# The rows of x of two attentions, transposed by TensorE or by DMA

## The reference

```
x = layernorm(x + causal_attention(x))          # weights with low-rank additions, output projection
h = ln1(x + self_attention(x));                  # "self": queries, keys, values all from x
h = ln2(h + cross_attention(h, context))
h = ln3(h + relu(h @ fc1 + b1) @ fc2 + b2)
x = layernorm(x + h)
x = layernorm(x + bit_ffn(x))                    # quantized activations and weights, gelu
```

## Time and profile before

| | us |
|---|---|
| median of 3 runs | 3415.64 (3407.46 to 3430.44) |
| profiled execution, its own time | 3414.83 |
| its span, first to last instruction | 3413.0 |
| mean granted TensorE clock | 0.974 of full speed |

### The profile page before, as it was taken

The page is one execution under the profiler, slowest core; times in us unless marked ns, Lnnn a source line. Parts: engine busy times, 40 slices in busy tenths (PEclk is TensorE's granted clock), DMA queues, the critical chain, the costliest instruction groups (busy, mean ns, idle before and its releaser), DMA issues.

```text
span 3413.0 us, 88599 instructions
## 1 busy us (share of the span) xinstructions
PE 3142.6 (92%) x35500; PEld 2438.5 (71%) x35500; DVE 2618.3 (77%) x4755; ACT 1999.8 (59%) x4522; POOL 1227.4 (36%) x1128
## 2 busy tenths in 40 slices
PE   7999999998999869999999999999989999999996
PEld 4888888877889747777777777777765656556562
DVE  5777788888889758888888888888875666666666
ACT  2665566666667626667677666667773444435442
POOL 0444421136665652443344333334212222222122
PEclk9999999999999889999999999999999999999998
DMA  3566655436554544555445545554343112221212
GB/s 99 171 185 217 184 156 161 135 116 196 160 164 136 161 118 119 125 130 127 119 123 133 129 121 126 129 124 107 84 153 105 48 49 53 50 53 44 54 38 52
DMA packets 445189, 405.71 MB, mean 119 GB/s; under 512 B 270471, under 2 KB 352523, under 8 KB 443630
## 3 DMA queue, kind: packets, MB, share of 16 engines
q1 hardware_dynamic: 444526, 399.78, 43.3%
q10 hardware_dynamic: 256, 0.26, 0.0%
HBM read 239.72 MB, written 109.52 MB: 102 GB/s over the span
## 4 chain that ended last, share of the span: by engine, by line
PE 55%; DMA 13%; DVE 13%; SPq 8%; ACT 5%; issue 4%; POOL 1%; ACTq 0%; POOLq 0%; DVEq 0%
PE at_ps L746 23%; PE at_ps L890 5%; PE at_ps L870 4%; PE at_ps L833 4%; PE at_ps L1393 4%; PE at_ps L1407 3%; DMA causal_spill<-at_proj 3%; PE at_ps L1418 3%; DMA self_spill<-at_proj 3%; PE at_ps L1372 2%; DVE at_mx_cross L953 2%; SPq L702 2%; DMA at_w_first<-cross_spill 2%; DMA at_o_raw<-at_values 2%; PE at_ps L775 2%
## 5 line engine op out<-in xcount | busy, mean ns | idle before, releaser
L960 DVE TENSOR_TENSOR at_p<-at_ps,at_p 125x448 f16<-125x448 f32 (+1 forms) x1280 | 781.6, 617 | 181.2 <-ACT at_ps L913 171.6
L912 ACT ACTIVATE at_p<-at_ps 125x448 f16<-125x448 f32 (+1 forms) x1280 | 698.4, 546 | 374.1 <-PE at_ps L870 352.6
L913 ACT ACTIVATE at_ps<-at_ps 125x448 f32<-125x448 f32 (+1 forms) x1280 | 699.8, 547 | 0.0
L953 DVE TENSOR_REDUCE at_mx_cross<-at_ps 128x1 f32<-128x750 f32 x512 | 476.2, 930 | 58.2 <-PE at_ps L833 57.0
L1033 POOL TENSOR_TENSOR at_o_sum<-at_o_raw 128x256 f32<-128x256 f32 x192 | 121.5, 633 | 919.8 <-ACT at_o_raw L919 907.3
L870 PE MATMUL at_ps<-at_stacks 97*112 97x224 f16 (+2 forms) x1792 | 338.5, 258 | 18.6 <-DMA at_stacks<-at_mrow 17.0
L890 PE MATMUL at_ps<-at_values,at_p 112*128 112x33 f16 (+3 forms) x7168 | 315.7, 185 | 13.5 <-ACT at_o_raw L919 7.4
L905 ACT ACTIVATE at_proj<-at_ps 128x448 f16<-128x448 f32 (+2 forms) x320 | 154.9, 484 | 276.5 <-PE at_ps L746 276.4
L956 DVE TENSOR_REDUCE at_mx<-at_ps 128x2 f32<-128x448 f32 x512 | 304.3, 610 | 7.8 <-PE at_ps L845 6.5
L890 PEld LDWEIGHTS at_ps<-at_values,at_p 112*128 112x128 f16 (+1 forms) x7168 | 284.6, 97 | 33.9 <-ACT at_o_raw L919 10.1
L1372 PE MATMUL at_ps<-at_xt,at_early 128*128 128x256 f16 x1792 | 299.8, 274 | 6.1 <-ACT at_w_first L1442 5.1
(11 more groups left out here) (202 smaller groups left out, 6753.3 us busy)
## 6 DMA issues: line engine op xcount, KB each, us to landing
at_x_res<-x SPq DMA_DIRECT2D x124, 256.0 KB, 3.0
cross_spill<-at_proj SPq DMA_DIRECT2D x64, 487.0 KB, 2.9
at_x_rows<-x SPq DMA_DIRECT2D x92, 256.0 KB, 4.4
at_prep<-bit SPq DMA_DIRECT2D x32, 512.0 KB, 4.6
at_early<-ctx SPq DMA_DIRECT2D x32, 512.0 KB, 4.0
at_stacks<-cross_spill SPq DMA_DIRECT2D x64, 243.5 KB, 3.6
causal_spill<-at_proj SPq DMA_DIRECT2D x64, 224.0 KB, 2.0
at_stacks<-causal_spill SPq DMA_DIRECT2D x128, 112.0 KB, 2.3
```

The lines of the kernel that those rows point to most:

```text
L912: act.activation(mem.p_hi[0:self.KC, n % 4, :], scores, ACT.Exp, scale=EXP_SCALE)
L913: act.activation(scores, scores, ACT.Exp, scale=EXP_SCALE).then_inc(self.exp_done, 1)
L953: dve.tensor_reduce(self.mx[:, at, t, h:h + 1], mem.ps_qk[:, :, 0:self.KT // 2], AX.XY, ALU.max).then_inc(self.max_done, 1)
L960: dve.tensor_tensor(mem.p_lo[0:self.KC, n % 4, :], mem.ps_st[0:self.KC, self.st_bank(b, g, n), 0:2 * T], mem.p_hi[0:self.KC, n % 4, :], AL ...
```

## The change

For batches 2 to 31, x is no longer transposed on TensorE. `split x` makes the high part of the rows as they lie (112 partitions x 1024 columns) on ScalarE and the low part on VectorE, into `x_parts`; x0 and x1 are each one DMA transpose on SP. TensorE, ScalarE and VectorE return from x0 and x1 at once, and these take no PSUM bank. Batches 0 and 1 stay as they were. The rows are loaded three batches ahead, as 2 x 112 rows. In the lists load moves from step 0 to the end of step 1 (causal) and into step 2 behind stack (self); splitx stands in step 0 (causal) and step 1 (self); x0 and x1 stand side by side near the start of step 2. At the change to the cross attention its first GpSimd split comes two steps later. The counts that semaphores are waited for change with it.

```diff
     "causal":
-  0: "... M2 V1 v0a M3 E0 V2 v0b load S0 V3"
+  0: "... M2 V1 v0a M3 E0 V2 v0b splitx S0 V3"
-  1: "... V1 E0 M2 spill ot0 stack S0 V2 ot1 M3 V3"
+  1: "... V1 E0 M2 spill ot0 stack S0 V2 ot1 M3 load V3"
-  2: "E1 S1 S2 x0 M0 V0 qka S3 V1 qkb M1 spill S0 E0 y0a y0b x1 M2 M3 V2 v0a v0b stack y1a y1b row V3"
+  2: "E1 S1 S2 x0 x1 M0 V0 qka S3 V1 qkb M1 spill S0 E0 y0a y0b M2 M3 V2 v0a v0b stack y1a y1b row V3"
     "self":
-  0: "M0 S1 residual load S2 E1 qka M1 S3 qkb V0 spill ..."
+  0: "M0 S1 residual S2 E1 qka M1 S3 qkb V0 spill ..."
-  1: "... M2 spill M3 V1 E0 v0b V2 V3 stack apply S0"
+  1: "... M2 spill M3 V1 E0 splitx v0b V2 V3 stack apply S0"
-  2: "x0 S1 S2 M0 E1 qka qkb V0 S3 V1 M1 E0 v0a v0b spill x1 stack V2 V3 M2 M3 S0 row"
+  2: "S1 S2 x0 x1 M0 E1 qka qkb V0 S3 V1 M1 E0 v0a v0b spill stack load V2 V3 M2 M3 S0 row"
...
+    def dma_inputs(self, b):
+        return b >= 2
...
-        elif self.cross and kind in ("x0", "x1"):
+        elif kind in ("x0", "x1") and self.dma_inputs(b):
             t = int(kind[1])
             if t == 0:
-                sp.wait_ge(self.x_split, b - self.b0 + 1)
+                sp.wait_ge(self.x_split, b - 1)
                 sp.wait_ge(self.proj_full, self.back(b, 2).projected(b - 2))
             to = mem.xt[:, b % 2].rearrange("p i c t -> p (i c) t")
             sp.dma_start(to[:, :, t * T // 2:(t + 1) * T // 2], mem.x_parts[:, t].rearrange("p i d -> p (i d)"),
                          transpose=True).then_inc(self.xt_in[b % 2], 16)
...
     def scalar(self, act, kind, b, g, n):
...
+        elif kind == "split x" and not self.cross:
+            act.wait_ge(self.x_rows_in[b % 2], 32 * (b // 2 + 1))
...
+            act.mul(mem.x_parts[:, :, 0, :], mem.x_rows[0:T // 2, b % 2, :, :], S_ACT).then_inc(self.x_hi_done, 1)
...
     def vector(self, dve, kind, b, g, n):
...
+        elif kind == "split x" and not self.cross:
+            dve.wait_ge(self.x_hi_done, b - 1)
+            dve.scalar_tensor_tensor(mem.x_parts[:, :, 1, :], mem.x_rows[0:T // 2, b % 2, :, :], S_ACT,
+                                     mem.x_parts[:, :, 0, :], ALU.mult, ALU.subtract).then_inc(self.x_split, 1)
```

More of the change, by code:

```diff
@@ L505, in __init__, with is_job @@
         self.UNSPLIT_JOBS = ["y0", "y1", "row"]
-        self.ALL_JOBS = ([] if self.cross else self.IN_JOBS) + self.OUT_JOBS + self.UNIT_JOBS + ["row"]
+        self.ALL_JOBS = self.IN_JOBS + self.OUT_JOBS + self.UNIT_JOBS + ["row"]
         self.full_index, self.hi_index, self.free_index = jobs.full_index, jobs.hi_index, jobs.free_index
     def index_job(self, kind, b, g, n):
-        if kind in self.ALL_JOBS and n != "first half":
+        if self.is_job(kind, b) and n != "first half":
             self.jobs.add(self, (kind, b, g), True, kind not in self.UNSPLIT_JOBS)
+    def dma_inputs(self, b):
+        return b >= 2
+    def is_job(self, kind, b):
+        return kind in self.ALL_JOBS and not (kind in self.IN_JOBS and self.dma_inputs(b))
     def halves_of(self, kind, b, g):
@@ L571, in inputs_in @@
     def inputs_in(self, b, kind):
-        if not self.cross:
+        if not self.dma_inputs(b):
             return [self.released("x1", b, 0)]
-        turn = (b - self.b0) // 2 + 1
-        return [(self.xt_in[b % 2], 32 * turn) if kind == "q" else (self.ct_in[b % 2], 96 * turn)]
+        if kind in ("q", "qk") or not self.cross:
+            return [(self.xt_in[b % 2], 32 * (b // 2))]
+        return [(self.ct_in[b % 2], 96 * ((b - self.b0) // 2 + 1))]
     def projected(self, b):
@@ L642, in sync @@
                 sp.wait_ge(self.stored, 32 * (b - self.NB + 1))
-            if b >= 2 and self.back(b, 2).cross:
-                sp.wait_ge(self.x_split, b - 1 - self.b0)
+            if self.dma_inputs(b - 2):
+                sp.wait_ge(self.x_split, b - 3)
             elif b >= 2:
@@ L647, in sync @@
             for t, q0 in enumerate(TILES):
-                rows, q0 = (T // 2, t * T // 2) if self.cross else (P, q0)
+                rows, q0 = (T // 2, t * T // 2) if self.dma_inputs(b) else (P, q0)
                 sp.dma_start(mem.x_rows[0:rows, b % 2, t, :], self.x_in[b - self.b0, q0:q0 + rows, :]
@@ L673, in sync @@
             if c == 0:
-                sp.wait_ge(self.proj_full, before.full_index["x1", self.b0 - 2, 0] + 1 if b == self.b0 else
+                sp.wait_ge(self.proj_full, before.full_index["qk", self.b0 - 2, 0] + 1 if b == self.b0 else
                            before.last_projected() if b == self.b0 + 1 else self.projected(b - 2))
@@ L782, in tensor @@
         KC, KT, NCH = self.KC, self.KT, self.NCH
+        if kind in self.IN_JOBS and self.dma_inputs(b):
+            return
         if kind in self.ALL_JOBS:
@@ L898, in scalar @@
         mem, HALF = self.mem, self.HALF
-        if n == "first half":
+        if n == "first half" or kind in self.IN_JOBS and self.dma_inputs(b):
             return
@@ L913, in scalar @@
             act.activation(scores, scores, ACT.Exp, scale=EXP_SCALE).then_inc(self.exp_done, 1)
+        elif kind == "split x" and not self.cross:
+            act.wait_ge(self.x_rows_in[b % 2], 32 * (b // 2 + 1))
+            if b == 2:
+                act.wait_ge(self.first_weights.w_lo_done, 8)
+            else:
+                act.wait_ge(self.xt_in[(b - 1) % 2], 32 * ((b - 1) // 2))
+            act.mul(mem.x_parts[:, :, 0, :], mem.x_rows[0:T // 2, b % 2, :, :], S_ACT).then_inc(self.x_hi_done, 1)
         elif kind == "evacuate":
@@ L1006, in gpsimd @@
         if kind == "split x":
+            if not self.cross:
+                return
             pool.wait_ge(self.x_rows_in[b % 2], 32 * (b // 2 + 1))
-            if at >= 1:
-                pool.wait_ge(self.xt_in[(b - 1) % 2], 32 * ((at - 1) // 2 + 1))
+            pool.wait_ge(self.xt_in[(b - 1) % 2], 32 * ((b - 1) // 2))
             rows = mem.x_rows[0:T // 2, b % 2, :, :]
             pool.tensor_scalar(rows, rows, S_ACT, 1.0, ALU.mult, ALU.mult).then_inc(self.x_hi_done, 1)
-            pool.wait_ge(self.x_hi_done, 2 * at + 1)
+            pool.wait_ge(self.x_hi_done, self.b0 - 2 + 2 * at + 1)
             pool.tensor_scalar(mem.x_parts[:, :, 0, :], rows, 1.0, 1.0, ALU.mult, ALU.mult).then_inc(self.x_hi_done, 1)
-            pool.wait_ge(self.x_hi_done, 2 * at + 2)
+            pool.wait_ge(self.x_hi_done, self.b0 - 2 + 2 * at + 2)
             pool.tensor_tensor(mem.x_parts[:, :, 1, :], rows, mem.x_parts[:, :, 0, :], ALU.subtract
@@ L1315, in sync @@
             if b < 2:
-                sp.wait_ge(cross.x_split, cross.NB)
+                sp.wait_ge(cross.x_split, cross.b_end - 2)
             else:
@@ L1705, in step @@
                 elif kind in ("load", "loadc"):
-                    at = resolve(b + (3 if layer.cross else 2))
+                    at = resolve(b + 3)
                     what = ("load" if kind == "load" else "load c", n)
@@ L1745, in start @@
                 yield causal, "scores", 0, 0, n
+            yield from loads(2)
         def spread(work, among):
```

6 lines of the change are left out of this document (3 added, 3 removed), and 12 rows, old and new, of the table ORDERS.

## The result

The changed kernel takes 3470.1 us (median, 3461.0 to 3475.9) beside 3421.1 us for the kernel before in the same comparison (3407.5 to 3430.4): a ratio of 1.0164, 95% interval 1.0134 to 1.0194, so 49 us slower by the medians. The profiled execution has a span of 3472.1 us against 3413.0.

What follows compares the result with a forecast made beforehand. Bound by TensorE where SP is on time, by SP's chain of spill, landing and stack where late. Self +4, causal after weight splitting -6, causal before +8 gave +6 us: 3422 us, own range 3396 to 3448, with rivals 3362 to 3465.

Steps and rivals of the forecast that it cites:

- What TensorE gets back: Eight transposes fewer per batch on TensorE: 0.88 us per batch, 26.4 us over 30 batches; 36 us as upper bound.
- the third rival: TensorE's saved time returns as waits for VectorE, so nothing of note changes: 3415 us; chance 0.44 together with the forecast.
- The 11.3 us for the rows of x: Causal wait of TensorE for x rows disappears with x0; only 4 us counted as gain, bounds 0 and 11.3.
- ScalarE and VectorE: Split replaces removed work on both engines, net -0.03 us each per batch; taken as 0, other bound 18 us.
- Self, the landing of the spill behind the transposes: Self step 2, without preparation: spill behind transposes lands at 1054.4 to 1055.8; new S0 wait 0 to 3.2 us, 1.2 taken.
- the lower end: Self step 2: the spill does not queue behind the transposes and lands at 1054.4.
- Self, the load's leaving: Self batches beside preparation: load leaves the spill's front in step 0; M0's wait shrinks 1.5 us, bounds 0.9 and 2.3.
- Self, where the new wait stands: Self batches beside preparation: load and transposes in step 2 make S0 wait 2.7 us for the row, bounds 1.2 and 4.
- The last line of "what would show it": Signs of error: L870's waits staying near 12 us, or TensorE regularly waiting for at_p or the transposed x.
- Causal: Nine batches beside weight splitting: row 2.2 us late each, +8 us in all with x_rows; seven later batches -6 us.
- the first rival: SP's queue has room and the self stall goes, with a third of lost clock: 55 us gained, 3360 us; chance 0.27.
- The slower rival: Spill lands behind x1 in most batches, so S0 of step 3 waits for the row everywhere: +45 us, 3461 us; chance 0.29.

Runs made afterwards that it cites:

- e12: Kernel before with DMA transposes in self attention only, issued in step 1, rows' loads and self residual load behind the row of maxima; 3378.4 us, 0.9909.
- e13: Kernel before, TensorE transposing all x, with rows loaded three batches ahead and behind the row of maxima, self residual load also behind it; 3375.9 us, 0.9898.
- e4_tiny_split: Changed kernel with only 8 of 512 columns of x split from batch 3 to the end of self attention; 3467.2 us, 1.0157.
- e1_early: Changed kernel with x0 and x1 moved one step earlier, to step 1 in front of the stack, in both lists; 3426.0 us, 1.0027.
- e3_load_back: Changed kernel with the rows' load put back in step 0 in both lists, still three batches ahead; 3483.8 us, 1.0210.
- e10_both: e7_self_only with the causal row of maxima of step 2 moved ahead of the stack; 3397.2 us, 0.9959.
- e7_self_only: Kernel before with DMA transposes in self attention only, issued in step 1, and rows loaded three batches ahead, behind the row of maxima; 3384.7 us, 0.9916.
- e8_row_before_stack: Changed kernel with transposes in step 1, loads behind the row of maxima, and the causal row of step 2 ahead of the stack; 3388.9 us, 0.9928.

## Why the prediction was wrong

It said 3422 us, slower within what a measurement can tell, with a range to 3465. It is 3470. Of the 53 us by which the spans differ more than forecast (59 against 6), 30 are in the causal stage (31.7 against 2), 19 in the self stage (23.3 against 4) and 4 behind them. Two terms that the sum had at nothing made them: in self the wait for the transposed x, in causal the slower clock. By its steps:

- **What TensorE gets back**, 0.88 us a batch: right in kind, too large. By the undisturbed batches of e12 and e13 it is 0.65 us. In the changed kernel the causal batches after the splitting of weights show the same: the store of y starts at 515.73 and, three batches on, at 625.55, 36.6 us each, against 37.25 us in e13, which has TensorE's transposes there (501.15 to 612.89). There PE is busy for 1.03 us a batch less, and a wait of 0.6 us a batch for VectorE's softmax, which e13 lacks, takes a part back: the third rival, in small. Over 30 batches 0.65 us is 20 us and not 26.4.
- **The 11.3 us for the rows of x**: they went, and a wait of 9.0 us for the transposed x came in the same stage. I took 4. With the load three ahead and behind the row but TensorE transposing, the causal stage shrinks by 16 us (e13, 632.7 against 648.6), so the load's move was worth more than I gave it there, and the DMA transposes hid that.
- **ScalarE and VectorE**: right, net nothing (1.047 and 1.225 us an instruction; e4_tiny_split).
- **Self, the landing of the spill behind the transposes**: the lower end was right in size (2.2 us at 905.16), by the mechanism of the upper one. The rule cited from the Trainium skill (DMA: Bandwidth & Descriptors, Queues, rings and completion order), that descriptors of a ring are consumed in order, agrees with the trace: each of the 30 spills landed behind the second transpose. What was mis-sized is the transpose, in 3.1 us after its issue in the self attention where I took 4.3, with the spill issued 1.4 us after it. A spill behind the rows' load lands as close behind its load (0.5 to 0.6 us in e1_early's causal batches), and that load takes longer.
- **Self, the load's leaving**: right. The spill's wait went from 27.3 to 7.9 us, and e3_load_back brought it back.
- **Self, where the new wait stands: this is the step that failed.** I made the row of maxima, read by S0 of step 3, what is late next, 2.7 us beside the preparation. It waited 4.9 us in all (650 to 1200 us). Late was the transposed x itself: 38.3 us in 11 waits, for which my sum had nothing. I costed what stands behind the transposes in the queue and never asked who reads them, nor behind what they stand. The reader, qka, runs five units ahead of the work, in the very next step, and the stack in front of them waits for a late spill. The last line of "what would show it" names this case. e1_early, which moves only them, took the self stage from 566.6 to 531.8 us. Self by parts, over the whole stage: +43 (transposed x, with a twelfth wait at 1200 us), -19 (spill), +4 (row of maxima), +4 (a wait for VectorE's at_mrow) and -9 (0.65 us in 14 batches) is +23, as measured.
- **Causal**: the right wait in the right place (12.1 to 35.9 us, where I asked for 40 or more in all), 24 us more over 11 waits against my 2.2 late in nine. **The step that failed here is the clock**, which the sum left out: 0.99 to 0.95, 22 us by the records. I had priced the clock for a gain, in the first rival, and not for a loss. Causal by parts: +24 (row), +9 and -11 (x), +22 (clock) and some -10 (0.65 us in 16 batches) is +34, beside 31.7 measured.
- **The slower rival** was nearest, at 3461. Its condition held, as the spill lands behind x1 in every batch, and its 3.5 us in nine causal batches, 31.5 us, is near the 24 of the row. But its wait of 3 to 4 us in each self batch is not there (4.9 us in all): that it came so near to 3470 is in part luck, as the wait for the transposed x and the clock, neither of them in it, filled the gap.

What stays open: why e10_both is slower than e7_self_only in the self stage; and whether the 7 us that e12 loses at the change to the cross attention is regular.

The best versions, e12 and e13 at 0.991 and 0.990 of the kernel before, owe it to the order of loads on SP. In e13 the transposes by DMA are not there, so they are not needed for that. How much of it is the load's place and how much its going three batches ahead was not separated.

## What to carry to other kernels

When work moves from an engine to DMA, find the first reader of the result and the instruction in front of it on the issuing queue, before costing what stands behind it: a transfer that is ready 7 us early is still late if a queue that waits for something else holds it. Put bulk loads behind the small transfers that others wait for; that, with the rows loaded a batch earlier, was worth 1% here, and the transposes added nothing to it that can be told. Waits of a bound engine can eat what the change gives back to it, and they went with a slower clock on top.

## What the runs showed of the hardware

- A spill issued on SP's queue right behind two DMA transposes landed 0.44 to 0.68 us after the second of them in 29 of 30 batches, 2.2 us after its own issue in the self attention and 2.8 in the causal one (medians); one right behind the 2 DMAs of the rows' load took 4.9 us (e1_early, median of ten), one with nothing just ahead of it some 2.0.
- TensorE's granted clock from 100 to 650 us was 0.95 with 36 us of waits for the row of 1.6 to 5.8 us, and 0.99 with as many transposes, more DMA traffic (0.68 against 0.63 busy) and one such wait (e8_row_before_stack).
- Issuing the transposes from ScalarE took the wait for them from 38.3 us to 0.3 in the self attention and put 15.8 us of waits for ScalarE in its place.
